# Messages scattered as three bf16 planes, and VectorE's two-operand work beside scatters cut into pieces, in a four-layer graph kernel

## The reference, cut to what matters

```
def spline_conv(x, row, col, basis, idx, W, b):
    z = jnp.einsum('ni,kio->nko', x, W).reshape(N * K, Fout)
    gathered = z[col[:, None] * K + idx]
    msg = jnp.einsum('es,eso->eo', basis, gathered)
    out = jax.ops.segment_sum(msg, row, num_segments=N)
    deg = jax.ops.segment_sum(jnp.ones_like(msg[:, 0]), row, num_segments=N)
    return out / jnp.maximum(deg, 1.0)[:, None] + b
...
basis, idx = spline_basis(pseudo)
h = jnp.ones((N, 1), x.dtype)
h = jax.nn.elu(spline_conv(h, row, col, basis, idx, stn1_w, stn1_b))
h = jax.nn.elu(spline_conv(h, row, col, basis, idx, stn2_w, stn2_b))
...
basis2, idx2 = spline_basis(new_pseudo)
return spline_conv(x, row, col, basis2, idx2, conv_w, conv_b)
```

## Time and profile before

| | us |
|---|---|
| median of 3 runs | 10544.22 (10543.03 to 10548.49) |
| the profiled execution | 10548.12 |
| its span | 10546.3 |
| POOL busy | 6510.9 (62%) |
| PE busy | 6169.8 (59%) |
| DVE busy | 5914.7 (56%) |
| ACT busy | 2150.7 (20%) |

### The profile page before, as it was taken

One profiled execution on the slowest core, in us unless ns is written; L12 is line 12 of the kernel. 1 busy time (PEld: TensorE's weight loads), 2 busy tenths in 40 slices (PEclk: granted clock), 3 DMA queues, 4 the chain that ended last, 5 costly groups with the idle time before them and its releaser, 6 DMA issues. The chain is left out here.

```text
span 10546.3 us, 181138 instructions
## 1 busy us (share of the span) xinstructions
PE 6169.8 (59%) x49368; PEld 5217.4 (49%) x49369; DVE 5914.7 (56%) x12028; ACT 2150.7 (20%) x5870; POOL 6510.9 (62%) x6754
## 2 busy tenths in 40 slices
PE   5552056666677776666556566645554555555565
PEld 5442035555677764444444555334444444445554
DVE  8993076555566658888695645731111333367645
ACT  0000024444333331111103140011111111124140
POOL 3777727777677776777443146357777777765140
PEclk9999987887555558888656575665555555557575
DMA  6993012222433321111285656682000111125655
GB/s 212 303 117 26 5 50 85 84 85 77 112 104 104 104 84 47 54 54 53 53 186 177 155 212 166 139 59 27 14 14 9 28 28 28 28 44 207 143 217 119
DMA packets 1315177, 1004.33 MB, mean 95 GB/s; under 512 B 894007, under 2 KB 1157419, under 8 KB 1306047
## 3 DMA queue, kind: packets, MB, share of 16 engines
q1 hardware_dynamic: 954526, 648.46, 26.7%
q0 software_dynamic: 225216, 279.29, 8.5%
q10 hardware_dynamic: 135264, 74.60, 3.1%
HBM read 495.63 MB, written 546.44 MB: 99 GB/s over the span
## 5 line engine op out<-in xcount | busy, mean ns | idle before, releaser
L2823 POOL DMA_INDIRECT msg<-msg,idx x1792 | 1743.2, 973 | 593.1 <-issue 528.6
L1166 POOL DMA_INDIRECT run_rows<-rec,idx x544 | 598.9, 1101 | 1108.3 <-ACT rec L1144 979.6
L2653 POOL DMA_INDIRECT cell<-rec,idx x944 | 936.5, 992 | 509.9 <-issue 284.1
L2373 POOL DMA_INDIRECT cell<-rec,idx x944 | 971.6, 1029 | 334.5 <-issue 286.7
L2034 POOL DMA_INDIRECT rec_d<-rec,idx x880 | 881.6, 1002 | 452.2 <-issue 267.1
L511 POOL DMA_INDIRECT rec_r<-sc_rec,sc_idx x832 | 885.7, 1065 | 431.7 <-issue 286.4
L2803 PE MATMUL ps<-w_stn,hft 128*128 x1792 | 599.1, 493 | 405.0 <-ACT hft L2757 401.9
L2590 PE MATMUL ps<-h_rows,oht 128*128 x1888 | 450.9, 403 | 547.3 <-ACT oht L2597 546.8
L826 DVE TENSOR_TENSOR oh<-iota_f,rd 128x512 f32<-128x512 f32 x237 | 167.3, 708 | 1023.1 <-PE ps L2575 1022.4
L2590 PEld LDWEIGHTS ps<-h_rows,oht 128*128 128x128 f32 x1888 | 420.3, 328 | 640.8 <-issue 640.8
L2803 PE MATMUL ps<-w_conv,hft 128*128 x1792 | 438.4, 426 | 499.8 <-ACT hft L2757 499.8
(11 more groups left out here) (455 smaller groups left out, 15787.6 us busy)
## 6 DMA issues: line engine op xcount, KB each, us to landing
loc<-loc_s SPq DMA_DIRECT2D x68, 2048.0 KB
got<-run_rows SPq DMA_DIRECT2D x472, 224.0 KB
got<-rec_d SPq DMA_DIRECT2D x236, 416.0 KB
rec_d<-padd SPq DMA_DIRECT2D x4, 12480.0 KB
rec_d<-padd SPq DMA_DIRECT2D x4, 12064.0 KB
cin<-cell SPq DMA_DIRECT2D x224, 136.0 KB
cell<-rec,idx POOLq DMA_INDIRECT x1888
loc<-loc_d ACTq DMA_DIRECT2D x118, 256.0 KB
```

Of the source, the lines that this page charges most:

```text
L1166: nc.gpsimd.indirect_dma_start(out=out, out_offset=bass.IndirectOffsetOnAxis(ap=idx[:, u, m % HU:m % HU + 1], axis=0), in_=rec[:, m, :], i ...
L2373: nc.gpsimd.indirect_dma_start(out=cells, out_offset=bass.IndirectOffsetOnAxis(ap=idx[:, n, g:g + 1], axis=0), in_=rec[:, n, g, :], in_off ...
L2653: nc.gpsimd.indirect_dma_start(out=cells, out_offset=bass.IndirectOffsetOnAxis(ap=idx[:, n, g:g + 1], axis=0), in_=rec[:, n, g, :], in_off ...
L2823: nc.gpsimd.indirect_dma_start(out=msgs, out_offset=bass.IndirectOffsetOnAxis(ap=idx[:, n, g:g + 1], axis=0), in_=msg[:, n, g, :], in_offs ...
```

## The change

Three things are done.

1. In `messages` the split into three bf16 terms is made before the scatter. `msg` stays f32 on the chip; ScalarE casts it to the high plane (`highest`), VectorE subtracts (`remainder`), ScalarE casts the rest to the middle plane (`middle`), VectorE subtracts again (`lowest`). A scattered row is now 3(F+1) bf16 values: 392 bytes for F = 64 (before 260) and 200 for F = 32 (before 132). The ring of rows and indices has U = 8 batches, and VectorE finishes, subtracts and subtracts again 1, 2 and 3 batches behind. The reduction L2727 becomes additions in pieces of 128 elements, and `hf` is made in four pieces.
2. `sum_messages` serves both sums, without any split: VectorE only makes the one-hot. For F = 32 the first two planes go in one matmul of 66 columns and the third in one of 33, and seven additions at the end join them; for F = 64 it is three matmuls as before. Addresses are read 20 at a time.
3. Operations of VectorE with two operands in SBUF that run beside scatters are cut into pieces of 128 elements (`hots_by_tile`, `rank_hot`, `rank_position`; L2091 and L2097 into four of 180), and L1106 into pieces of 512.

```diff
+        MW1, MW2 = (-(-3 * (F + 1) // 2) for F in (F1, F2))
-        msg1 = dram("msg1", (P * TILES_N, F1 + 1))
+        msg1 = dram("msg1", (P * TILES_N, MW1))
...
-            nc.vector.tensor_tensor(sel, sel, s["hot"][:, m, :, :, :], ALU.mult).then_inc(s["s_sel"], 1)
+            for B in s["parts"]:
+                taken = nc.vector.tensor_tensor(sel[:, :, B, :], sel[:, :, B, :], s["hot"][:, m, :, B, :], ALU.mult)
+            taken.then_inc(s["s_sel"], 1)
...
+        def hots_by_tile(oh, local):
+            for g in range(G):
+                made = nc.vector.tensor_tensor(oh[:, g, :], iota_f[:, :], bcast(local[:, g:g + 1], [P, P]), ALU.is_equal)
+            return made
...
                                 for w in range(SUPER):
-                                    made = nc.vector.tensor_scalar(hot[:, m % RING, w, :], loc[:, u, m % HU, :], lane_c[:, w:w + 1], None,
-                                                                   ALU.is_equal)
+                                    for e in (slice(0, HR * P), slice(HR * P, RUN * P)):
+                                        made = nc.vector.tensor_scalar(hot[:, m % RING, w, e], loc[:, u, m % HU, e], lane_c[:, w:w + 1], None,
+                                                                       ALU.is_equal)
...
-                            hot_of(oh[:, n % RING, :, :], got[:, n, :, XW + MLOC]).then_inc(s_hot, 1)
+                            hots_by_tile(oh[:, n % RING, :, :], got[:, n, :, XW + MLOC]).then_inc(s_hot, 1)
...
-                                nc.vector.tensor_tensor(mid[:, n, :, :], got[:, n, :, :], upper(got, n), ALU.subtract).then_inc(s_mid, 1)
                                 one_hot(oh[:, n, :, :], rl, k * G, 0).then_inc(s_hot, 1)
-                                v.wait_ge(s_mid, k + 1)
-                                nc.vector.tensor_tensor(low[:, n, :, :], mid[:, n, :, :], upper(mid, n), ALU.subtract).then_inc(s_low, 1)
...
-                            nc.vector.tensor_reduce(msg[:, n, :, 0:F], wy[:, n % 2, :, :, :].rearrange("p g c o -> p g o c"),
-                                                    AX.X, ALU.add).then_inc(s_msg, 1)
+                            if rest == 4:
+                                for g in range(G):
+                                    to = wy[:, h, g, 0:2, :]
+                                    made = nc.vector.tensor_tensor(to, to, wy[:, h, g, 2:4, :], ALU.add)
+                                made.then_inc(s_msg, 1)
+                                v.wait_ge(s_msg, ADDS * k + 1)
+                            v.wait_ge(s_left, k + 1)
+                            for B in halves_g:
+                                made = nc.vector.tensor_tensor(msg[:, n, B, :], wy[:, h, B, 0, :], wy[:, h, B, 1, :], ALU.add)
+                            made.then_inc(s_msg, 1)
+                        def remainder(i, m):
+                            v.wait_ge(s_high, k + 1)
+                            v.wait_ge(s_low, k + 1)
+                            for B in halves_g:
+                                made = nc.vector.tensor_tensor(left[:, n, B, :], msg[:, n, B, :], planes[m][:, B, 0, 0:F], ALU.subtract)
+                            made.then_inc(s_left, 1)
+                        def lowest(i, m):
+                            v.wait_ge(s_mid, k + 1)
+                            for B in halves_g:
+                                made = nc.vector.tensor_tensor(planes[m][:, B, 2, 0:F], left[:, n, B, :], planes[m][:, B, 1, 0:F], ALU.subtract)
+                            made.then_inc(s_low, 1)
+                        def highest(i, m):
+                            act.wait_ge(s_msg, ADDS * (i * U + m + 1))
+                            nc.scalar.copy(planes[m][:, :, 0, 0:F], msg[:, m % R, :, :]).then_inc(s_high, 1)
+                        def middle(i, m):
+                            act.wait_ge(s_left, i * U + m + 1 + R)
+                            nc.scalar.copy(planes[m][:, :, 1, 0:F], left[:, m % R, :, :]).then_inc(s_mid, 1)
```

More of the change, by code:

```diff
@@ L412, in rank_rings @@
             J = upto.shape[1]
-            s = dict(bank=bank, upto=upto, J=J)
+            s = dict(bank=bank, upto=upto, J=J, parts=[slice(g, g + 2 // J) for g in range(0, G, 2 // J)])
             s["hot"], s["sel"] = sb_in(c, "bin_hot", [P, R, J, G, CELLS], BF16), sb_in(c, "bin_sel", [P, 2, J, G, CELLS])
@@ L2560, in _ @@
                         v.wait_ge(s_kept, ABANKS2)
+                        if paired:
+                            for q in range(ABANKS2):
+                                nb = min(PER_BANK2, NB - q * PER_BANK2)
+                                to = acc[:, q * PER_BANK2:q * PER_BANK2 + nb, :]
+                                nc.vector.tensor_tensor(to, to, ps[:, q, 0:nb * PITCH].rearrange("p (b w) -> p b w", w=PITCH)[:, :, W:2 * W],
+                                                        ALU.add).then_inc(s_kept, 1)
+                            v.wait_ge(s_kept, 2 * ABANKS2)
         def pick_rings(c):
@@ L2600, in pick_hot @@
             v.wait_ge(s["turned"], k + 1)
[L2601 removed]
+            hots_by_tile(s["oh"][:, n, :, :], rd[:, ds(t, G), LOC]).then_inc(s["hot"], 1)
         def to_cells(nodes, pitch, F, cells, load_weights, blank):
@@ L2667, in messages @@
             K = TILES_C // G
-            NIC = TILES_C // STEP
+            NIC = K // U
+            assert NIC * U == K and U % R == 0
             banks = -(-G * rest * F // 512)
@@ new lines, in lowest, with back @@
+                        def lowest(i, m):
+                            k, n = i * U + m, m % R
+                            v.wait_ge(s_mid, k + 1)
+                            for B in halves_g:
+                                made = nc.vector.tensor_tensor(planes[m][:, B, 2, 0:F], left[:, n, B, :], planes[m][:, B, 1, 0:F], ALU.subtract)
+                            made.then_inc(s_low, 1)
+                        def back(what, i, m, by, first):
+                            if m >= by:
+                                what(i, m - by)
+                            elif not first:
+                                what(i - 1, m - by + U)
@@ new lines, in turn @@
+                        def turn(i, first, last):
+                            for m in range(U):
+                                if m + 2 < U:
+                                    prepare(i, m + 2)
+                                elif not last:
+                                    prepare(i + 1, m + 2 - U)
+                                back(finish, i, m, 1, first)
+                                back(remainder, i, m, 2, first)
+                                back(lowest, i, m, 3, first)
@@ L2750, in _ @@
+                        remainder(NIC - 1, U - 1)
+                        lowest(NIC - 1, U - 2)
+                        lowest(NIC - 1, U - 1)
                     @block.scalar
@@ new lines, in middle, with turn @@
+                        def middle(i, m):
+                            act.wait_ge(s_left, i * U + m + 1 + R)
+                            nc.scalar.copy(planes[m][:, :, 1, 0:F], left[:, m % R, :, :]).then_inc(s_mid, 1)
+                        def turn(i, first, last):
+                            for m in range(U):
+                                number(i, m, first)
+                                if m + 1 < U:
+                                    copy_turned(i, m + 1)
+                                elif not last:
+                                    copy_turned(i + 1, 0)
+                                if m >= 1:
+                                    highest(i, m - 1)
+                                elif not first:
+                                    highest(i - 1, U - 1)
+                                if m >= 2:
+                                    middle(i, m - 2)
+                                elif not first:
+                                    middle(i - 1, m - 2 + U)
@@ L2787, in turn @@
                         def turn(i, last):
-                            for n in range(R):
-                                k, t = i * R + n, i * STEP + n * G
-                                if not last or n < R - 1:
-                                    turn_h(k + 1, (n + 1) % R, False)
-                                ids = block_ids(ENG.PE, "c", t, WMAX)
+                            for m in range(U):
+                                k = i * U + m
+                                if m + 1 < U:
+                                    turn_h(i, m + 1)
+                                elif not last:
+                                    turn_h(i + 1, 0)
+                                ids = block_ids(ENG.PE, "c", k * G, WMAX)
                                 pe.wait_ge(s_copy, k + 1 + R)
@@ L2823, in _ @@
                                     nc.gpsimd.indirect_dma_start(
-                                        out=msgs, out_offset=bass.IndirectOffsetOnAxis(ap=idx[:, n, g:g + 1], axis=0),
-                                        in_=msg[:, n, g, :], in_offset=None,
```

(8 more changed lines are left out.)

289 lines of the change are left out of this document (110 added, 179 removed).

## The result

The changed kernel takes 10472.22 us (median of 5 runs, 10454.05 to 10495.69), the kernel before 10544.22 beside it (10540.6 to 10561.0). The ratio is 0.9933, with an interval of 0.9913 to 0.9952: faster by 72 us. The forecast was 10407 (10320 to 10480), so the sign and the range hold and the gain is half of what was worked out. The time lies 8 us inside the upper end of the range, where the prediction had put rival (a), and (a) is not what happened: that it still falls inside is luck. The runs also spread over 42 us where those of before spread over 20.

What follows compares the result with a forecast made beforehand. Each stage has its own limit: POOL's scatter descriptors in six stages, VectorE in the F = 64 sum, PE's sequence in the last. Terms sum to −137 us, 10548.1 to 10411, less 4 for the median: 10407, range 10320 to 10480.

Steps and rivals of the forecast that it cites:

- rival (a): First messages: VectorE's step passes POOL's 5.11 us; at 5.3 to 5.8 it costs 43 to 155 us; chance 0.09.
- Pieces release POOL: Stages with scatters: POOL gets in between VectorE's pieces, leaving about 0.2 of a loss; rank stage −56 us, `to_cells` −16.
- Rival (e): Rank stage, both passes, `to_cells`: POOL gets no gap between pieces, +70 us where −126 stood, total 10603; chance 0.02.
- send_runs, -24: `send_runs`: halves of the one-hot shorten holds, −24 us, at most −50, nothing if PE's chain sets the pace.
- the square law: Expected scatter loss goes by the square of VectorE operation length less 0.17; in `send_runs`, 0.20 becomes 0.13.
- Destination-order pass, -39: Destination-order pass: 55 us of excess, nearly all by 236 one-hots; cutting these gives −39 us.
- Sum, F = 64, -35: Sum for F = 64: PE's sequence is next but transfers come close; 309 us becomes 274, −35, range −70 to 0.
- The 283 us: Sum for F = 64: time for 71 MB of transfers, 31 MB in 150 us and 40 in 133.
- Last sum, -3: Last sum: fewer address loads save 15 us, slower batches may take it; −3 us, range −40 to +5.
- Messages, +35 and +16: Both `messages` stages: pipeline start and pieces in flight cost +35 us for F = 64 and +16 for F = 32.
- (b): First messages: short pieces do not overlap, VectorE's step nears 6.1 us, +220 us, total about 10630; chance 0.04.
- Rival (c): VectorE does not hold scatters; rank stage, both passes and `to_cells` give nothing (−126 less), total 10533; chance 0.03.

## Why the prediction was right in sign and wrong in size

- **Pieces release POOL.** Right for the rank stage, -58 of -56, and `to_cells`, -22 of -16, where the scatters' own time fell by 56 and 17 us. (The rest of the 22, and the 15 us by which the rank stage moved without pieces, are pauses that the forecast did not treat.) The source-order pass gave -9 of -15. The step that failed is the word "so" behind the earlier trace rows: from one timeline, where four pieces of 125 let POOL in after 0.10, I took it that POOL is released between pieces always. The trace held the counterexample, the scatter of 25.96 us. (The 0.17 us read from the earlier trace rows is 0.13: the one-hot ends at 7097.06, 0.65 after the scatter's start, and the loss is 0.52.) In `send_runs` 75 halves in a row shut it out, in the destination-order pass four products now and then. Rival (e) had this mechanism, at 0.02, but for all stages at once; in truth it was one stage and a half.
- **send_runs, -24.** It came to +50. The estimate of 0.35 for a half was good (0.343 is the median of the trace; 0.622 the longest), the square law was not, since it takes holds one by one. The upper bound "nothing if PE's chain sets the pace" left out that it could cost. This is 74 of the 83 us between the forecast for the profiled execution and the measured one.
- **Destination-order pass, -39.** It came to -5 in this trace, -5 to -18 in the others. The hold moved to the products; with a wait after each product the full -39 came.
- **Sum, F = 64, -35.** It came to -23, in other kernels up to -51. That transfers and PE come next was right in kind, and the run without the fill shows the transfers as the limit. The 283 us were no bound, since two kernels took 244: I had read 207 GB/s at a share of 1.12 as near the limit, and at the same share the changed kernel moves 228 and the one with whole one-hots in `send_runs` 260. PE's 1.03 us a batch was too high: it does 220 batches in 200 us. (The two queues of the earlier trace rows add up to 56.4 MB and not 56.7, which moves nothing.)
- **Last sum, -3.** It came to -28. I took PE's sequence for the limit from the earlier trace rows, although had VectorE busy for 224.55 of 230 us. VectorE's four batches take 4.01 us without a gap, as long as the cycle of 2.69 + 1.32 that I gave to PE. The 0.67 a batch "set by these steps" was too high as well: PE does the same twelve matmuls in 0.58 later, and why it took 0.67 is open.
- **Messages, +35 and +16.** They came to +24 and +6. VectorE's step was worked out at 5.01 us and measures 4.70: the changed kernel starts `fb` at 3925.71 and again at 3930.41, and the wait behind the four additions costs 0.03 us where I had put 0.21. So it stays under POOL's 5.11 with 0.4 to spare, and rivals (a) and (b) fall. The start cost 10, as said; the pieces in flight 15, as said (973 to 989 ns).
- **Rival (c)**, that VectorE does not hold scatters and these stages stay, falls: with the same count of scatters, those of the rank stage got 67 ns shorter each with the pieces, and with the pieces undone they are back at 1065. The rule of the Trainium skill's page "SBUF — State Buffer", section Who interferes with whom, by which a `tensor_tensor` does not stall descriptor generation, does not agree with this: a row of such operations held a scatter for 0.84 us.
- The rule of the Trainium skill's page "VectorE: DVE Perf Modes", section The TRN2 errata, to keep tiles at 512 elements or more, was weighed by its price for VectorE alone, and that price was paid beside POOL's time, as forecast. It would not have warned of `send_runs`: the halves there have 512 elements, which the rule allows.

## What to carry to other kernels

If VectorE holds up POOL's scatters, cutting its operations is half of the cure: an unbroken row of pieces can hold a scatter longer than one whole operation does. A wait of VectorE for its own last piece breaks the row and costs about 0.1 us a time; look for the longest scatter in the trace, not at the mean, and never leave outliers aside. Before a stage's limit is worked out anew, read which engine is at 98% in it now; and when a stage's engine work is taken away, ask what runs beside it on the transfers and could run elsewhere.

## What the runs showed of the hardware

- A scatter (floor 0.97 us) next to VectorE on bf16 `tensor_scalar`: beside 22 whole operations of 1024 elements in a row it takes up to 1.28 us (but beside 16 of them 4.04), beside 75 halves in a row 19.76 us, beside the same halves with a pause after every four 0.98 on average and 1.11 at most. Beside one-hots and subtractions of f32 inputs in one row until 5415.55 it took 25.96. With four products of f32 in a row, 1.82 in the changed kernel and, where it started in the one-hot's last piece ahead of them, 2.11 (kernel with the moved fill); with eight in a row, up to 2.10.
- A wait of VectorE for the end of its last product lengthens four of them from 1.16 to 1.53 us.
- The share of the DMA engines' time does not tell what they move: at 1.12 in the same stage, 207, 228 and 260 GB/s in three kernels.
- The same kernel takes 10535 to 10544 us in three series on at least two chips and 12527 on another, where POOL waits for some 4 us about every 19 in the destination-order pass, while a stage without scatters has the same length (`sum_runs`, loads of `run_rows` to one sum, 195 us on both).
